# A cross-attention layer on one core: the last scores, the last transposes and the layer norm take other places in the round

## What is computed

```python
# block 0; x (4,256,256), xf (4,256,256); H=16 heads of K=128; F=1024
def cross_attention(q_in, kv_in, wq, bq, wk, bk, wv, bv, wo, bo, bias_k, bias_v):
    qh = (q_in @ wq + bq).reshape(b, q_len, H, K)
    kh = (kv_in @ wk + bk).reshape(b, t, H, K)
    vh = (kv_in @ wv + bv).reshape(b, t, H, K)
    kh = concatenate([kh, bias_k]); vh = concatenate([vh, bias_v])   # one more key and value
    weights = softmax(einsum('bqhk,bthk->bhqt', qh, kh) / sqrt(K))
    return einsum('bhqt,bthk->bqhk', weights, vh).reshape(b, q_len, H * K) @ wo + bo
x = x + cross_attention(layer_norm(x), xf, ...)     # twice, with other weights
x = x + gelu(layer_norm(x) @ w_fc1 + b_fc1) @ w_fc2 + b_fc2
```

## Time and profile before

| | |
|---|---|
| median of 3 runs | 1309.03 us (1307.08 to 1309.49) |
| the profiled execution | 1308.19 us, its span 1306.5 us |
| granted TensorE clock, mean | 0.963 |
| busy share of the span | PE 89%, PEld 69%, DVE 65%, ACT 49%, POOL 50% |
| layer 0's rounds 0 to 15 | from 32.4 to 699.6 us of the span |

### The profile page before, as it was taken

The page is one execution under the profiler, slowest core; times in us unless marked ns, Lnnn a source line. Parts: engine busy times, 40 slices in busy tenths (PEclk is TensorE's granted clock), DMA queues, the critical chain, the costliest instruction groups (busy, mean ns, idle before and its releaser), DMA issues. The chain is left out here.

```text
span 1306.5 us, 20609 instructions
## 1 busy us (share of the span) xinstructions
PE 1167.3 (89%) x7388; PEld 903.0 (69%) x7388; DVE 850.1 (65%) x2097; ACT 638.9 (49%) x1428; POOL 656.2 (50%) x677
## 2 busy tenths in 40 slices
PE   5999999999999999999989859976758998899994
PEld 4788888888888878888778724433436775666664
DVE  5776676766757666667656364995545666676756
ACT  3655555555655555455652114203223673477770
POOL 3655665666646565466762023670012661277760
PEclk9999999999999999999999979998788999899997
DMA  6110221112210121012202000000030000000000
GB/s 205 64 51 17 65 65 49 32 51 65 66 49 19 64 65 49 26 57 65 65 18 80 1 16 1 0 1 1 0 90 1 2 2 2 1 1 2 2 2 33
DMA packets 35110, 47.05 MB, mean 36 GB/s; under 512 B 3865, under 2 KB 22082, under 8 KB 35010
## 3 DMA queue, kind: packets, MB, share of 16 engines
q1 hardware_dynamic: 34640, 44.83, 10.7%
q10 hardware_dynamic: 370, 0.91, 0.2%
HBM read 44.69 MB, written 1.05 MB: 35 GB/s over the span
## 5 line engine op out<-in xcount | busy, mean ns | idle before, releaser
L444 POOL TENSOR_TENSOR a_prob<-a_prob,a_inv_total 128x512 f32<-128x512 f32 x128 | 144.3, 1128 | 216.2 <-DVE a_inv_total L732 216.2
L1583 POOL TENSOR_TENSOR l_scores<-l_scores,l_neg_max 128x512 f32<-128x512 f32 x144 | 147.9, 1042 | 99.4 <-DVE l_neg_max L1573 99.2
L1573 DVE CUSTOM_DVE_ANT_0 l_scores<-psum,mask 128x256 f32<-128x256 f32 x384 | 139.8, 421 | 69.6 <-PE psum L1526 69.6
L637 ACT ACTIVATE a_prob<-psum,a_neg_max 128x257 f32<-128x257 f32 x256 | 119.2, 472 | 92.8 <-DVE a_neg_max L729 91.9
L1604 ACT ACTIVATE l_prob_T<-psum 128x512 f32<-128x512 f32 x192 | 108.8, 590 | 34.3 <-PE psum L1540 34.2
L1540 PE MATMUL psum<-ident,l_scores 128*128 128x128 f32 x768 | 116.4, 290 | 7.0 <-POOL l_scores L1583 3.9
L1540 PEld LDWEIGHTS psum<-ident,l_scores 128*128 128x128 f32 x768 | 85.1, 145 | 41.1 <-issue 18.8
L736 DVE TENSOR_TENSOR a_probT_lo<-psum,a_probT_hi 128x512 fp32r<-128x512 f32 x128 | 87.9, 686 | 23.1 <-ACT a_probT_hi L641 22.6
L729 DVE TENSOR_REDUCE a_neg_max<-psum 128x2 f32<-128x514 f32 x128 | 87.2, 681 | 1.3 <-PE psum L486 1.3
L566 PE MATMUL psum<-ident,a_prob 128*128 128x128 f32 x512 | 77.6, 274 | 6.9 <-POOL a_prob_bias L447 6.9
L641 ACT ACTIVATE a_probT_hi<-psum 128x512 fp32r<-128x512 f32 x128 | 76.7, 600 | 9.3 <-PE psum L566 9.3
(11 more groups left out here) (331 smaller groups left out, 3296.6 us busy)
## 6 DMA issues: line engine op xcount, KB each, us to landing
wk_raw<-in_L_xattn_wk SPq DMA_DIRECT2D x16, 512.0 KB, 6.4
wq_raw<-in_L_xattn_wq SPq DMA_DIRECT2D x16, 512.0 KB, 5.7
wv_raw<-in_L_xattn_wv SPq DMA_DIRECT2D x16, 512.0 KB, 3.8
wo_raw<-in_L_xattn_wo SPq DMA_DIRECT2D x16, 512.0 KB, 4.0
ctx_rows<-in_ctx SPq DMA_DIRECT2D x3, 512.0 KB, 4.3
x_rows<-in_x SPq DMA_DIRECT2D x2, 512.0 KB, 9.5
mask<-in_mask_Bx1xSxS_ff SPq DMA_DIRECT2D x1, 1024.0 KB, 7.9
out_dram<-fin_y SPq DMA_DIRECT2D x4, 256.0 KB, 2.1
```

The source lines that it names most:

```text
L444: pool.tensor_tensor(prob[:, m % 4, :, 0:S], prob[:, m % 4, :, 0:S], rtot[:, m % 4, :].unsqueeze(2).to_broadcast([P, 2, S]), ALU.mult)
L637: act.activation(prob[:, m % 4, q, 0:S + 1], s_bank(g)[:, q, 0:S + 1], ACT.Exp, bias=negm[:, m % 4, q:q + 1], accum_out=tot[:, m % 4, q:q ...
L1573: e = dve.tensor_tensor_reduce(sc[:, i % SC, q, :], s_bank(i)[:, q * S:(q + 1) * S], masks[:, b * NM + q % NM, :], 1.0, BIG, ALU.add, ALU. ...
L1583: pool.tensor_tensor(sc[:, i % SC, :, :], sc[:, i % SC, :, :], m[:, i % SC, :].unsqueeze(2).to_broadcast([P, 2, S]), ALU.subtract).then_in ...
```

## The change

It has six parts.
1. In rounds 0 to 14, S7 stands right behind K1 (before: behind A1).
2. T6 stands between Q2 and Q3, T7 between Q3 and K2 (before: T6 behind Q3, T7 behind K2). K3 stands at the end, behind A3 (before: ahead of A2). `key_columns` is issued behind K2.
3. The scores' wait for all of the last round's Q and K at S0 is split: S0, S2, S4 and S6 each wait for the Q and K of their own head.
4. X and Y are cut in four pieces, one for each tile of 128 rows, in place of two. X0 to X3 stand behind T1 to T4 in rounds with `i % 4 == 0`, Y0 to Y3 in the same places in rounds with `i % 4 == 1` (before, both stood in rounds with `i % 4 == 1`). A tile's mean and variance (`bn_aggr`) follow one piece later.
5. POOL makes 1/sqrt at the end of rounds with `i % 4 == 0`.
6. L0 stands behind S0 and L1 behind S2 in rounds with `i % 4 == 2` (before: behind V1 and V2).

The last round's own list is as it was.

```diff
-    base = ("S0 S1 O0 S2 O1 V0 T0 V1 S3 V2 T1 S4 V3 Q0 T2 S5 Q1 K0 T3 S6 K1 A0 T4 A1 "
-            "S7 T5 Q2 Q3 T6 K2 T7 K3 A2 A3").split()
+    base = ("S0 S1 O0 S2 O1 V0 T0 V1 S3 V2 T1 S4 V3 Q0 T2 S5 Q1 K0 T3 S6 K1 S7 A0 "
+            "T4 A1 T5 Q2 T6 Q3 T7 K2 A2 A3 K3").split()
...
-        if i % NQ == 1:
-            order = put(order, 'V1', 'X0')
-            order = put(order, 'V3', 'X1')
-            order = put(order, 'T3', 'Y0')
-            order = put(order, 'T4', 'Y1')
+        if i % NQ < 2:
+            for t in range(HT):
+                order = put(order, f'T{t + 1}', 'XY'[i % NQ] + str(t))
         if i % NQ == 2:
-            order = put(order, 'V1', 'L0')
-            order = put(order, 'V2', 'L1')
+            order = put(order, 'S0', 'L0')
+            order = put(order, 'S2', 'L1')
...
-                    if i % NQ == 1:
-                        rstd_of(event_of(i))
...
                     norm(7)
+                    if i % NQ == 0:
+                        rstd_of(event_of(i))
...
                             if m == 0:
                                 pe.wait_ge(vec_ok, 2)
-                                pe.wait_ge(acc_free, USE[i - 1, 'K3'] + 1)
-                                pe.wait_ge(acc_free, USE[i - 1, 'Q3'] + 1)
                                 pe.wait_ge(kcols, i + 1)
+                            if b == 0:
+                                pe.wait_ge(acc_free, max(USE[i - 1, f'Q{h}'], USE[i - 1, f'K{h}']) + 1)
...
+                            dve.bn_stats(bn[:, m, :], chip.x[:, t0 + m, :]).then_inc(ln_stat, 1)
+                            if m:
+                                aggregate(e, m - 1)
+                            if m == HT - 1:
+                                aggregate(e, m)
                                 dve.wait_ge(ln_aggr, HT * (e + 1))
                                 dve.tensor_scalar(ve[:, :], mv[:, :, 1], EPS0, None, ALU.add).then_inc(ln_var, 1)
...
-                                if m == QUAD - 1:
+                                if m == 2:
                                     key_columns(i + 1)
```

More of the change, by code:

```diff
@@ L238, in put @@
         return order[:at] + list(new) + order[at:]
-    out = {-1: "C0 C1 X0 X1 K0 Y0 Y1 K1 L0 L1 K2 K3 Q0 Q1 Q2 Q3".split()}
+    out = {-1: "C0 C1 X0 X1 X2 X3 K0 Y0 Y1 Y2 Y3 K1 L0 L1 K2 K3 Q0 Q1 Q2 Q3".split()}
     for i in range(LOOPS):
@@ L249, in layer0_orders @@
             order = put(order, 'V3', 'B0')
-        if i % NQ == 1:
-            order = put(order, 'V1', 'X0')
-            order = put(order, 'V3', 'X1')
-            order = put(order, 'T3', 'Y0')
-            order = put(order, 'T4', 'Y1')
+        if i % NQ < 2:
+            for t in range(HT):
+                order = put(order, f'T{t + 1}', 'XY'[i % NQ] + str(t))
         if i % NQ == 2:
-            order = put(order, 'V1', 'L0')
-            order = put(order, 'V2', 'L1')
+            order = put(order, 'S0', 'L0')
+            order = put(order, 'S2', 'L1')
         out[i] = order
-    out[LOOPS] = "O0 O1 X0 X1 Y0 Y1 G0 L0 L1 G1 F0 F1 F2 F3 F4 F5 F6 F7 G2 G3".split()
+    out[LOOPS] = "O0 O1 X0 X1 X2 X3 Y0 Y1 Y2 Y3 G0 L0 L1 G1 F0 F1 F2 F3 F4 F5 F6 F7 G2 G3".split()
     return out
@@ L709, in key_columns, with aggregate @@
                     ins.then_inc(kcols, 1)
+                def aggregate(e, j):
+                    dve.wait_ge(ln_stat, HT * e + j + 1)
+                    dve.bn_aggr(mv[:, j, :], bn[:, j, :]).then_inc(ln_aggr, 1)
                 def query_weights(j):
@@ L743, in _ @@
                                 else:
[L744 to L750, removed]
+                                    dve.wait_ge(acc_free, USE[i, 'O1'] + 1)
+                            dve.bn_stats(bn[:, m, :], chip.x[:, t0 + m, :]).then_inc(ln_stat, 1)
[3 more added lines that the diff above has]
+                                aggregate(e, m)
                                 dve.wait_ge(ln_aggr, HT * (e + 1))
@@ L753, in _ @@
                         elif k == 'Y':
[L754 to L757, removed]
+                            if m == 0:
+                                dve.wait_ge(ln_rstd, e + 1)
+                            dve.tensor_scalar(xn[:, m, :], chip.x[:, t0 + m, :], mv[:, m, 0:1], rstd[:, m:m + 1], ALU.subtract, ALU.mult).then_inc(ln_norm, 1)
+                            if i < 0 and m == HT - 1:
                                 query_weights(0)
```

## The result

| | median, us | runs | ratio to before, 95% interval |
|---|---|---|---|
| before | 1308.05 (1306.62 to 1311.32) | 6 | |
| the changed kernel | 1318.69 (1316.59 to 1323.32) | 6 | 1.009, 1.0069 to 1.011 |

The change makes the kernel 10.6 us slower. That lies in the forecast's range and 2.8 us from its number. The profiled executions have spans of 1306.5 and 1316.6 us.

What follows compares the result with a forecast made beforehand. PE's stream was taken as the bound, with only its waits movable. The terms 26.7 - 4.6 + 6.1 + 0.4 - 6.6 (old X and Y waits) - 9.2 gave +12.8 us, forecast 1321.5, range 1313 to 1331.

Steps and rivals of the forecast that it cites:

- Q2 +0.42 and Q3 +1.2: Second half of a round: Q2 waits 0.42 us for A0's bank, Q3 1.2 us for A1's.
- the rival that A1's low part is not what PE waits for: At Q3: A1's bank is free by 350.9, so the edit gains 16 us, to 1293; chance 9%.
- the rival in which gain and loss cancel: Whole rounds: tail costs 0.9 a round with none of Q2's wait, X3 0.5; 1305 to 1311 us; chance 7%.
- the one in which POOL gets late: At T7: norm(7) pushed by more than 0.9, T7 waits too; 0.7 us a round more, 1332; chance 9%.
- K3 +0.25: Round's end: K3 waits for A2's bank, its low part delayed by the key columns on DVE; +0.25 us.
- The tail: Second half of rounds 0 to 14, from Q2 to K3: +1.78 us per round, +26.7 in all.
- O0 -0.38: Start of the next round: O0 no longer waits for A3's low part; -0.38 us in 12 rounds, -4.6.
- The split gives nothing of its own: At S0: splitting the scores' wait saves nothing itself, but allows K3 to stand last.
- X +1.53 in rounds 0, 4, 8, 12: X's pieces delay Q1's, K1's and A1's low parts on DVE: +1.53 us in each of four rounds, +6.1.
- Y +0.1 a round: Rounds 1, 5, 9, 13: Y's pieces take 0.33 to 0.41 us each and cost 0.1 a round, +0.4.
- L -9.2: Rounds 2, 6, 10, 14: L beside O0 and O1, T7 waiting 1.2 for POOL; net -9.2 us, between -11.2 and -7.
- The clock, a rival with 2%: Rounds with X3: clock falls to 1.2 GHz for the rest, each losing up to 6 us: 1345; chance 2%.

Runs made afterwards that it cites:

- the parts that pay: Kernel before with split wait, L's new places, X and Y in four pieces one step earlier than the change, h_low ahead of norm(3): 1291.56 us, ratio 0.9871.
- the tail alone: Kernel before with parts 1 to 3 of the change (list of steps, split wait, key columns), layer norm as before: 1334.25 us, ratio 1.0185.
- the layer norm's places alone: Kernel before with parts 4 to 6 of the change (X, Y and L), old list, wait and key columns: 1298.1 us, ratio 0.993.
- S7 back: Changed kernel with S7 back behind A1; T6, T7 and K3 keep their new places: 1316.11 us, ratio 1.0062.

## Why the prediction was right

**PE is the bound and only its waits move.** Right, with the clock beside it: wherever a round's length was taken apart here, PE's waits and the falls of the clock make up the difference.

**Q2 +0.42 and Q3 +1.2.** Measured 0.40 and 1.18. Moving E7 alone takes Q3's part away. The mechanism of the largest term is shown, and the rival that A1's low part is not what PE waits for is refuted. Q2's wait is there, against the rival in which gain and loss cancel, and T7 has none in round 7, against the one in which POOL gets late.

**K3 +0.25.** Wrong, it is 0. The failed step is "the key columns, now behind K2, hold DVE until 358.15 (1.09 and 0.16, less overlaps)". The 1.09 was no property of the instruction. It lasted until POOL's cut ended; behind K2 POOL is idle and it takes 0.17. The forecast moved an instruction and took its duration along. The tail comes to 1.4 a round (1.03 in plain rounds and O0's 0.38) instead of 1.78, so 15 x 0.37, some 5.5 us, were forecast too much, the largest error in the rounds. K3 is the largest part of it; A3's wait (0.16 for 0.3) and the 0.02 each at Q2 and Q3 go the same way.

**O0 -0.38.** Right: O0's wait of 0.22 and its slower start are gone.

**The split gives nothing of its own.** Wrong by 1.6 us in one place: at round 0. There Q0 to Q3 stand last in the start's list and S0 waited 1.77 for Q3's low part. The rounds were read (K3 last) and the start was not. For the other rounds the sentence is right, as is "with the old wait S0 would stand 1.75 longer" (1.61).

**X +1.53 in rounds 0, 4, 8, 12.** Q3's wait was forecast near 2.7; it was 2.01 of idle, 2.26 by the starts. Beside the tail's 1.4, rounds 4, 8 and 12 leave 1.2 to 1.3 for X. The small sum's 1.05 us were on the path, as counted.

**Y +0.1 a round.** Too small. In round 1 Q3 waits 0.24 longer than in a plain round; in round 5 it is 1.0 in all, since K1 and Q2 wait too. A piece of 0.33 to 0.41 was forecast; one of them in round 5 takes 1.07, beside POOL's norm:

```profile
261.81 1.07 DVE L757 TENSOR_SCALAR ctx_rows<-x_rows,a_ln_mean_var,a_ln_rstd 128x256 f32<-128x256 f32 x1
...
261.69 1.04 POOL L442 TENSOR_TENSOR a_prob<-a_prob,a_inv_total 128x512 f32<-128x512 f32 x1
```

**L -9.2.** Right in kind, and T7's wait for POOL was 1.03 of idle, 1.2 by the starts. Beside a tail of 1.4 less O0's 0.38, the four rounds gave 8.3 us in all. POOL's h_low, as the forecast said, hold T7; moving them frees it.

**The clock, a rival with 2%.** It fell once more in the rounds than before, in round 0 for 1.3 us, and not for the rest of a round in four of them. As a fall of the price of 1345 the rival did not come; as a cost it was left out of the sum and is in it. The granted clock of 1.00 for the rounds was a mean over 665 us, and it hid a fall. In round 15 of the kernel before, a step of the last list waits 2.12, and the clock is at 0.66 from 684 to 686 us and at 0.50 from 686 to 688:

```profile
684.31 0.53 PE L484 MATMUL psum<-a_hT_hi,a_wq_hi 128*128 128x512 f32 x1 [2.12 <-DVE a_q_hi L815]
```

With that row at hand, a wait forecast near 2.7 in four rounds deserved more than 2% and a term of its own.

**Sum.** The rounds came out 2.3 below the forecast, the start 2.9 below, and what stands behind round 15 2.5 above. The last two nearly cancel by luck. In the next kernel they may not: what stands behind round 15 moved by -0.3 to +5.4 us in these runs without an edit that counts there. Within the rounds there was luck too: of the 5.5 us too much for the tail, some 3 were made up by what the forecast had left out or had too small, the fall in round 0 (1.3) and Y in rounds 5 and 13 (0.9 each).

## What to carry to other kernels

Before a step is moved ahead, follow the whole chain that it needs (here scores, maximum, exponential, reciprocal, scaling, turning: 5.87 us) and see where it ends today; if the step stands exactly there, moving it up by one step costs that step, wherever the wait then shows. A piece of work that another engine puts in front of a PSUM bank's release costs as much as work on TensorE, once TensorE already waits for that bank (the sum of 1.05 us gave back 1.1 a round). And an instruction's duration is to be taken from a row in which the neighbours do what they will do after the move.

## What the runs showed of the hardware

**VectorE's small instructions end with POOL's.** A cast of 128x8, a sum of 128x4, a normalisation of 128x256, all with one SBUF input and SBUF output in 32 bits, took 0.17, 0.17 and 0.40 us where POOL was idle. Beside POOL they took 1.09, 1.05 and 1.07, and ended 0.02 to 0.15 us behind POOL's running instruction (358.00 and 357.97; 232.75 and 232.73; 262.88 and 262.73). In the run with the parts that pay, the same sum took 0.69, since it began later beside its POOL instruction, and ended with that. VectorE's work out of PSUM did not grow beside POOL: A1's low part takes 0.74 either way. Nor did the reciprocal and `bn_aggr` (0.17 each), nor `bn_stats` (0.41). The Trainium skill says so ("SBUF — State Buffer", section "Who interferes with whom"): copy, cast and tensor_scalar can run in a mode with two ports, one pair of which VectorE shares with GpSimd, and who comes second is blocked until the other has ended. These runs agree, and POOL was the first in each of the three cases.

**A wait of 2 us can lower the clock, and need not.** In rounds 0 to 14 of the profiled runs, 24 of PE's waits were of 2.0 to 2.5 us (four each in the changed kernel and in five others). At 13 of them, by their end or within 1.5 us behind it, the granted clock fell to 0.50 for 3.4 us. Behind the shorter ones of these rounds, up to 1.77, it fell at none. That is no rule for shorter waits, as round 15 shows: in three runs (the tail alone, the layer norm's places alone, S7 back) the clock fell there behind two waits of 0.5 and 0.7 to 0.8 us, 1.4 to 1.5 us apart. And of the 14 waits of 2.0 to 2.1 us in round 15, one in each profiled run, 10 had a fall within 1.6 us behind them. What decides stays open: at the same wait at the same step it fell in round 0 of the changed kernel and in rounds 4 and 12 of the one with h_low early.
